# Attention softmax sums: fewer pours and additions, three blocks counted raw on TensorE, maxima two steps earlier

## What is computed

```
q = heads(ln(x) @ Wq);  k, v = heads(ln(x) @ Wkv)          # once for short, once for long
scores = q k^T / sqrt(32)  (+ -|i-j| * (1 - decay) for short)
p = softmax(scores);  out = alpha * p_short v_short + (1 - alpha) * p_long v_long
x = x + out @ Wo
```

## Time and profile before

| | |
|---|---|
| median of three runs | 4766.27 us (4765.73 to 4774.77) |
| profiled execution, its own time | 4764.1 us |
| its span, first to last instruction | 4762.1 us |
| mean granted TensorE clock | 0.973 |
| TensorE matmuls busy | 4467.5 us (94%) |
| VectorE busy | 3788.4 us (80%) |
| GpSimd busy | 3088.7 us (65%) |
| ScalarE busy | 2982.2 us (63%) |

### The profile page before, as it was taken

The page is one execution under the profiler, slowest core; times in us unless marked ns, Lnnn a source line. Parts: engine busy times, 40 slices in busy tenths (PEclk is TensorE's granted clock), DMA queues, the critical chain, the costliest instruction groups (busy, mean ns, idle before and its releaser), DMA issues. The chain is left out here.

```text
span 4762.1 us, 157195 instructions
## 1 busy us (share of the span) xinstructions
PE 4467.5 (94%) x61452; PEld 2434.6 (51%) x61452; DVE 3788.4 (80%) x4400; ACT 2982.2 (63%) x5297; POOL 3088.7 (65%) x1236
## 2 busy tenths in 40 slices
PE   8999799999999999999999999999995899999998
PEld 3444244444444555444444444444442677777776
DVE  7657788888888888888888888888781688888887
ACT  3222377777777777777777777777774455555553
POOL 0000389898989898988989888889885333333332
PEclk9999699999999999999999999999997899999999
DMA  5444376767666667667767666676754000000000
GB/s 168 138 127 123 86 150 139 156 143 153 144 146 142 151 146 156 137 145 146 151 144 151 143 144 144 144 153 144 151 107 117 21 28 21 28 28 21 28 23 12
DMA packets 242106, 547.41 MB, mean 115 GB/s; under 512 B 71471, under 2 KB 145327, under 8 KB 200561
## 3 DMA queue, kind: packets, MB, share of 16 engines
q0 software_dynamic: 45792, 333.47, 35.4%
q1 hardware_dynamic: 195563, 203.94, 15.0%
q10 hardware_dynamic: 38, 0.08, 0.0%
HBM read 140.34 MB, written 62.16 MB: 43 GB/s over the span
## 5 line engine op out<-in xcount | busy, mean ns | idle before, releaser
L983 DVE TENSOR_REDUCE rowmax_parts<-scores_qk 128x1 f32<-128x1024 f32 x2048 | 2414.8, 1218 | 514.4 <-PE scores_qk L1068 509.7
L961 ACT ACTIVATE probs_T<-scores_kq 128x512 f32<-128x512 f32 x3840 | 2069.3, 602 | 535.0 <-PE scores_kq L1068 379.0
L868 POOL TENSOR_TENSOR probs_added<-probs_added,probs_T 128x2048 f32<-128x2048 f32 x446 | 2093.9, 4695 | 48.0 <-POOL probs_added L868 38.1
L1068 PE MATMUL scores_kq<-q_operand,k_operand 103*32 103x512 f16 (+3 forms) x13312 | 1239.5, 372 | 126.5 <-DMA q_operand_above<-negmax_T 68.8
L1068 PE MATMUL scores_qk<-k_operand,q_operand 96*32 96x512 f16 (+4 forms) x13312 | 1050.7, 373 | 27.9 <-DMA v_operand<-v_dram 14.2
L1150 PE MATMUL outputs_T<-probs_T,v_operand 128*32 128x512 f32 x7680 | 1029.1, 598 | 6.4 <-issue 5.6
L1068 PEld LDWEIGHTS scores_kq<-q_operand,k_operand 103*32 103x32 f16 x13312 | 396.5, 96 | 692.5 <-ACT probs_T L961 275.8
L1068 PEld LDWEIGHTS scores_qk<-k_operand,q_operand 102*32 102x32 f16 (+1 forms) x13312 | 385.9, 98 | 512.6 <-issue 229.8
L1758 PE MATMUL f_gate_up<-w_gate_up,xq_T 128*128 128x256 f16 (+1 forms) x4608 | 494.2, 266 | 7.6 <-DVE hidden L1649 6.5
L868 POOL TENSOR_TENSOR probs_added<-probs_T 128x2048 f32<-128x2048 f32 x64 | 292.0, 4563 | 292.4 <-DVE probs_T L1012 239.3
L1758 PEld LDWEIGHTS f_gate_up<-w_gate_up,xq_T 128*128 128x128 f16 x4608 | 421.0, 98 | 77.0 <-issue 24.3
(11 more groups left out here) (173 smaller groups left out, 4570.0 us busy)
## 6 DMA issues: line engine op xcount, KB each, us to landing
probs_poured<-probs_T POOLq DMA_DIRECT2D x318, 1024.0 KB, 8.7
qk_parts_dram<-qk_parts SPq DMA_DIRECT2D x96, 256.0 KB, 2.8
q_operand<-qk_parts_dram SPq DMA_DIRECT2D x192, 128.0 KB, 3.4
k_operand<-qk_parts_dram SPq DMA_DIRECT2D x192, 128.0 KB, 7.4
v_dram<-v_heads SPq DMA_DIRECT2D x16, 1024.0 KB, 6.4
v_operand<-v_dram SPq DMA_DIRECT2D x64, 256.0 KB, 6.7
sums_inverse<-sums_inverse_dram SPq DMA_DIRECT2D x64, 256.0 KB
q_operand_above<-qk_parts_dram SPq DMA_DIRECT2D x96, 128.0 KB, 4.1
```

What stands on the lines that cost most here:

```text
L868: nc.gpsimd.tensor_tensor(total, first, block_of(w, b), ALU.add).then_inc(added.sem, 1)
L961: nc.scalar.activation(block_of(w, kb)[:, qt * BANK:(qt + 1) * BANK], pb[:, ring_of(c) % BANKS, :], ACT.Exp).then_inc(expd.sem, 1)
L983: nc.vector.reduce_max(rowmax[:, w % 2, g // 2, g % 2:g % 2 + 1], half, AX.X).then_inc(maxed.sem, 1)
L1068: mm = nc.tensor.matmul(out[j:j + HD, :], lhsT[:, j:j + HD], rhs, start=start, stop=stop, skip_group_check=True)
```

## The change

Per unit the sums are divided otherwise. Four blocks are poured (1, 4, 7, 10), eight are added by GpSimd in seven additions (2, 3, 5, 6, 8, 9, 11, 12), and three are not summed at all: TensorE counts blocks 13 and 14 beside the additions' total, and block 15 beside the pours' total, into the same bank. VectorE joins nothing. GpSimd's order is a table that is no longer the blocks' own. The 15 blocks get their buffers by a table: block 15 has one alone, the other 14 share seven, so blocks b and b + 7 are in the same. The next unit's maxima are complete after step 7 and turned at step 8, and SyncE places them before it stores the inverse.

```diff
-ASTEPS = 10
+ASTEPS = 8
-JOIN = 4
-TURN_MAX = 10
+TURN_MAX = 8
-BY_DMA = (1, 6, 9, 12, 15)
-JOINED = (2, 3)
-BY_POOL = (3, 4, 5, 7, 8, 10, 11, 13, 14)
+BY_DMA = (1, 4, 7, 10)
+BY_POOL = (2, 3, 5, 6, 8, 9, 11, 12)
+RAW = {13: 0, 14: 0, 15: 1}
-POOL_ORDER = (1, 4, 5, 6, 7, 8, 9, 10, 11, 12, 13, 14, 15)
-WEIGH_BEHIND = 14
+POOL_ORDER = (1, 3, 5, 4, 6, 8, 7, 9, 11, 10, 12)
+WEIGH_BEHIND = 12
+ALONE = 15
+SLOT = {b: k % (PBUF - 1) for k, b in enumerate(b for b in range(1, KB) if b != ALONE)} | {ALONE: PBUF - 1}
...
-            return poured_sum[:, w % 2, :] if kb == 0 else probs[:, kb % PBUF, :]
+            return poured_sum[:, w % 2, :] if kb == 0 else probs[:, SLOT[kb], :]
...
                         for j in range(2):
                             pack_sums(*back, j)
-                        store_inverse(*back)
                     if after(w, n, last):
                         place_max(*after(w, n, last))
                     if back:
+                        store_inverse(*back)
                         spread_inverse(*back)
...
                     first = block_of(w, BY_POOL[0])
-                    wait_apart(pool, joined, joined.at(n, w + 1), passed)
                     wait_apart(pool, counted[0], counted[0].at(n, w - 1), passed)
...
-                u, b = (w, kb - PBUF) if kb > PBUF else (w - 1, kb + PBUF) if kb < PBUF else (w - 1, kb)
+                same = [b for b in range(1, KB) if SLOT[b] == SLOT[kb]]
+                u, b = (w, same[0]) if kb > same[0] else (w - 1, same[-1])
                 act.wait_ge(summed.sem, summed.at(n, u * KB + b + 1))
-                if b == JOINED[0]:
-                    act.wait_ge(joined.sem, joined.at(n, u + 1))
+                if b in RAW:
+                    act.wait_ge(counted[RAW[b]].sem, counted[RAW[b]].at(n, u + 1))
...
-            def join(w, n):
...
-                        if i == JOIN:
-                            join(w, n)
...
-                count(pb[:, COUNT_SLOTS[0] % BANKS, :], added_sum[:, w % 2, :], True, True).then_inc(counted[0].sem, 1)
+                bank = pb[:, COUNT_SLOTS[0] % BANKS, :]
+                for b in RAW:
+                    if RAW[b] == 0:
+                        count(bank, block_of(w, b), b == min(RAW), False)
+                count(bank, added_sum[:, w % 2, :], False, True).then_inc(counted[0].sem, 1)
...
-                count(pb[:, COUNT_SLOTS[1] % BANKS, :], poured_sum[:, w % 2, :], True, True).then_inc(counted[1].sem, 1)
+                bank = pb[:, COUNT_SLOTS[1] % BANKS, :]
+                count(bank, block_of(w, KB - 1), True, False)
+                count(bank, poured_sum[:, w % 2, :], False, True).then_inc(counted[1].sem, 1)
```

More of the change, by code:

```diff
@@ L696, in attend @@
         summed = Rises(sem("a_pv"), UNITS * KB, credit=1)
-        joined = Rises(sem("a_joined"), UNITS, credit=1)
         added = Rises(sem("a_added"), UNITS * ADDS, credit=1)
@@ L840, in _ @@
         def _(pool):
-            give_credit(pool, [maxed, expd, summed, joined, added, sums_out, merged, inv_stored, inv_spread, taken, weighed]
+            give_credit(pool, [maxed, expd, summed, added, sums_out, merged, inv_stored, inv_spread, taken, weighed]
                         + counted + packed + stored)
@@ L1005, in _ @@
                 max_pair(1, 0, g)
-            def join(w, n):
-                a, b = JOINED
-                dve.wait_ge(expd.sem, expd.at(n, (w * KB + b + 1) * NQ))
-                dve.wait_ge(summed.sem, summed.at(n, w * KB + b + 1))
-                nc.vector.tensor_tensor(block_of(w, b), block_of(w, a), block_of(w, b), ALU.add).then_inc(joined.sem, 1)
             def merge(w, n):
```

## The result

The changed kernel takes **4802.74 us** (median of 4 runs, 4788.19 to 4805.86), the kernel before 4766.0 us on the same chip: ratio 1.0068, with a 95% interval of 1.0051 to 1.0086. It is 0.7% slower; the forecast was 4763 us and no difference. The number lies inside the range, the direction was wrong.

A forecast was written before the change was run, and what follows sets the result against it. TensorE was taken as the bound, losing some 220 us to waits. 161.6 - 80 - 24 - 22 - 35 + 3 + 4.7 - 0.8 - 10 = -2.5 us, 4764 us as a median; 1 us off gave 4763 us, range 4730 to 4805.

The forecast's parts named there:

- What bounds it, and the counts: TensorE bounds the units, losing some 220 us to waits; three more counts per unit add 161.6 us.
- The refill behind the longer pause at step 4: ScalarE and VectorE running dry at step 4 and restarting: taken as nothing, at most 38 us.
- The maxima's way back, -80 and -24: Step 14's waits for the next unit's maxima all go, -80 us; the half clock behind them goes too, -24 us.
- The join, -22: VectorE no longer adds blocks 2 and 3, so TensorE's step 5 shortens by 0.35 us per unit: -22 us.
- Pours and buffers, -35 and +3: ScalarE's waits to overwrite poured blocks go, -35 us; pour 7, on the edge, costs +3 us.
- the 0.42 of the text: Share of ScalarE's waits for pours taken as TensorE's loss: 0.42 x 84 gave -35 us.
- the walk: Times of GpSimd's additions and pours through a unit: pour 7 lands at 39.1 us, block 14 wants its buffer at 39.0.
- Ends: Prologue +4.7 us for eight more chunks of maxima; -0.8 us at the end; last unit -10 us from its pours.
- 59 are neither removed nor added: Of TensorE's 220 us of waits in the units, 59 us, mostly waits for no semaphore, were taken to stay.
- 1 us off for the thinner traffic: A few of the remaining waits may shrink with one pour of five gone: 1 us taken off.
- rival 1: Pauses shrink too, as pours share the DMA engines with code fetches: 27 us less, 4736 us; chance 0.17.
- rival 3: Waits come back elsewhere: a third of the 161 us removed only moves, 54 us, 4817 us; chance 0.08.

The follow-up runs named there:

- e4: Changed kernel with all four pours cut to 16 of 2048 columns, so sums lack the rest of those blocks: 4700.23 us, ratio 0.9852.
- e6: Changed kernel with SyncE's operand loads held until chunk 12 of the next unit's scores, nothing left out: 4773.9 us, ratio 1.0008.
- e12: Changed kernel with pour 10 alone cut to 16 of 2048 columns, other pours whole: 4735.36 us, ratio 0.9920.
- e1: Kernel before with only the maxima's part changed: turned at step 8, placed ahead of the inverse's store; five pours stay: 4730.44 us, ratio 0.9912.
- e3: Changed kernel with the maxima back at step 10, still placed ahead of the inverse's store: 4764.59 us, ratio 0.9994.
- e9: Changed kernel with the maxima back at step 10 and the inverse's store again ahead of the maxima's DMAs: 4776.58 us, ratio 1.0025.
- e8: Changed kernel with maxima at step 10, block 14 added by GpSimd, block 13 joined into it by VectorE at step 15: 4723.48 us, ratio 0.9894.
- e5: Changed kernel with pour 1 held on GpSimd's queue until block 3's exponentials are there, nothing left out: 4776.84 us, ratio 1.0012.
- e10: Changed kernel with pour 1 alone cut to 16 of 2048 columns, other pours whole: 4777.5 us, ratio 1.0012.

## Why the prediction was right and wrong

- **What bounds it, and the counts.** Right. TensorE made 2520 records of counts for the first 63 units, 40 each, and the three new counts cost 158.5 us for 161.6. The last three of them stand in the last unit, so 159.0 of the 161.6 us lie in the 63 units. The units lost 220 us to waits by the prediction; by e4's scale (4 us left over in 2982.5) it is 3033.4 + 159.0 - 2982.5 + 4 = 214. The refill behind the longer pause at step 4 was rightly taken as nothing.
- **The maxima's way back, -80 and -24.** The waits went, and the half clock: one stretch of 6.8 us is left, of 14 with 61 us in all between 600 and 3583 us, and there is none in e4, e6 and e12. The reason given was enough and not needed. The sum credited the two steps and the swap, and e1 shows that these two remove the waits in the kernel before; but e3 and e9 show that beside the new pours they go without the two steps, and all but 12 us without the swap. So, as parts of the change, the two steps had a value of nothing and a price of 38 us that was not in the sum at all. That the clock came out right is in part luck: in e1 the waits for the maxima went and 37 of 61 us of half clock stayed, around waits for ScalarE and pauses. By the Trainium skill (TensorE: Matmul & The Clock Gate, HAM oscillation) idle gaps bring the half clock. The trace agrees for the long ones: the stretch that is left begins inside the longest pause, 5.3 us, while the next longest, 2.6 us, has none.
- **The join, -22.** The step returned to its own length in the trace (no excess in step 5), so it is right there; e8 shows that it would be wrong at another place.
- **Pours and buffers, -35 and +3.** Half wrong. Of 84.3 us of ScalarE's waits 39.4 stayed; by the 0.42 of the text that is 19 us gained for 32. By the time in the unit at which ScalarE stands, 24 of the 39 us are waits for pour 7, the one on the edge (issued at 30.5 in odd units and 32.3 in even ones, landed at 38.7 and 40.7, for 39.1 by the walk): about 10 us by the 0.42, for 3. The other 15 us are for pour 10: it was to take its 8.7 us and took 11.0 to 12.2, landing at 53 for "49 to 51". The operand loads are only a part of that, since with them out of the way (e6) it still took 9.4 to 11.4; the inverse's spreading, issued at 40 to 41 us, and in odd units the store of the outputs, issued at 41, run beside it too, and no run moved those. The walk had looked at GpSimd's queue and at buffers, never at what else uses the DMA engines at that time.
- **Ends.** The prologue was right: 553.8 for 549.4 us. The last unit was to get 7 us shorter, counts included; from its first product to its last count's end it took 56.0 us (3615.2 to 3671.25) for 54.0 (3582.8 to 3636.84). Its pours made ScalarE wait 3.54 and 7.11 us. What follows the attention was 10 us shorter, 1115 for 1125 us, which no term had. The two together are 8 us, as forecast, and that is luck: two errors that cancel.
- **The step that failed: "59 are neither removed nor added".** This is most of the error. The sum has 3033.4 + 159.0 - 161 + 3 - 1 = 3033.4 us for the 63 units, and they took 28 more. Of these, 21 are in this step: the sum has 62 us of loss in the changed kernel's units (59, and 3 for pour 7), the kernel 83. Of the rest, 6 are the 220 us that were 214, and 1 is the shrinking that did not come. The pauses have 9 us of the 21 (38.5 for 29.7), the pours' waits 13 (39.4 x 0.42 for 3). The sum took 1 us off for the thinner traffic, as if only its amount counted, and it is its place that counts. The mechanism was half written down, twice: rival 1 named code and pours on the same engines, with the sign the other way, and rival 3 gave 4817 us for waits that come back elsewhere, at a chance of 0.08, by engines that caught up, which is not how it came. Neither asked when a GpSimd with one pour and one addition fewer comes to pour 1, and beside what: in before it left at 8.6 us of an even unit and 11.4 of an odd one, in the changed kernel at 2.7. The walk gave it "10 us to spare" and looked no further. Holding it back gave 26 us (e5), holding the loads back 29 (e6), and leaving the maxima at step 10, which holds back both, 38 (e3).
- **Rival 1's shared engines.** By the Trainium skill (Trainium Kernel Development and Optimization, Key Constraints) the DMAs that SyncE, ScalarE and GpSimd issue run on the same 16 engines and interleave. The text said that no row showed a late fetch because of a pour. The runs now do: in the 63 units 32 pieces of code land over 10 us after the one before with the whole pours, 3 with the small ones (e4), and 38.5 us of pauses become none.
- **What stays open.** That the code's fetches are the link is argued, from 25 of 50 pauses in which one is landing; no run moved the fetches alone. The other pauses have no fetch beside them. Nor is a late piece enough: 67 land over 10 us after the one before in the kernel before, with pauses of 29.7 us, and e3 has 32 like the changed kernel. What differs is the place. In the first 6 us of a unit there are 22 such pieces in the changed kernel, 17 in e5, 11 in e6, and 1 each in e3, e12 and e4; why TensorE stands still for them there and less elsewhere was not tried out. And the changed kernel's median is 14.5 us above its profiled execution, which nothing here explains.

## What to carry to other kernels

A step that is moved earlier moves everything that waited for it, also on engines off the path: follow the release until it reaches a DMA, and ask what that DMA then runs beside. Large transfers hidden behind compute are not free, since small ones that somebody waits for (loads, a row of maxima, the engine's own code) run beside them; holding a transfer back until the others are through can be the faster schedule. When a change has several parts, run the ones that cost nothing to separate: here one part had been credited with a gain that the others bring without it, and was itself the loss.

## What the runs showed of the hardware

- 1 MB added by a DMA of GpSimd's queue takes 6.9 us at least, 9.1 at the median, 13.3 at most from issue to landing (changed kernel); one that adds 8 KB takes 2.0 us at the median (e4), and 4.8 to 5.5 us if issued on the heels of a 1 MB one (e10's pour 1).
- With these transfers TensorE, which uses no data of theirs at the time, pauses with no releaser for up to 5.3 us, 38.5 us in 63 units, and not at all when they are small (e4); 67 of the 102 us that go with the pours belong to the one in four that meets the operand loads.
- SyncE is slower at issuing too: 3.75 us for three loads beside a pour (changed kernel), 1.97 us without (e12).
- A DMA's wait in a queue is worth watching even where nobody on the path waits: GpSimd's 408 us of waits for the inverse in e3 are the better schedule's, its 75.5 us the slower one's.
